# Next batch's rows normalised by ScalarE, result stores issued by ScalarE, and the work around them rearranged

## The chip, the cores and the metric

One core of a Trainium2 chip runs the whole program. The metric is device microseconds of one execution; the figure of a kernel is the median of several. The engines are TensorE (PE in the profile, PEld for its weight loads), VectorE (DVE), ScalarE (ACT), GpSimd (POOL) and SyncE (SP), which here only issues DMAs.

## The reference

Eight batches of 512 rows of 256 (`x`) attend to 1024 context rows each; then comes a feed-forward layer with routed experts. Cut to what matters:

```python
x = x + tanh(g_xattn) * xattn(layernorm(x), ctx)      # x 8x512x256, ctx 8x1024x256
x = x + tanh(g_ffn) * ffn(layernorm(x))
# xattn: lat, ctx = layer_norm(latents), layer_norm(context)
#   q = lat @ Wq; k, v = split(ctx @ Wkv); k = rope(k)        16 heads of 64
#   a = softmax(clip(q @ k.T / 8, -11, 11)); return (a @ v) @ Wo + bo
# ffn: scores = sigmoid(x @ router_w.T)                       64 experts in 8 groups
#   choose 4 groups, in them 8 experts per row; weights normed to sum 1, times 2.5
#   routed = sum over the chosen e of w_e * (relu(x @ up_w[e])**2 @ down_w[e])   256 -> 128 -> 256
#   shared = relu(x @ shared_up_w)**2 @ shared_down_w                            256 -> 512 -> 256
#   return routed + shared
```

## The kernel before

The program runs in four stages. Times are microseconds from the start of the span.

**Setup** (0 to 74) turns weights and the first batch's rows.

**Attention** (74 to 1905, function `attention`) goes over 8 batches `b`, in each over 8 pairs of heads `p`, in each over 8 steps `c`. In a step each engine's program runs its function `step`: TensorE multiplies `scores` (L903) for one tile of 128 context rows and both heads, and `ps_o` (L968, the product with `v`) for an earlier tile; ScalarE takes the exp into `e` (L1047); GpSimd clips `e` in place (L1139); VectorE sums `e` into `e_sum` (L1287), from which TensorE makes the denominators (L976). Beside this the next pair's keys are made: TensorE `ps_k` (L944), VectorE two products with cosines and sines, GpSimd their sum `k_c` (L1131, at c = 2 and 6), ScalarE the high part `k_t` (L1073), VectorE the rest of it (L1277). Batches 2 to 7 are one loop body, `Fori(2, B)`; batches 0 and 1 are written out.

Two more things are woven in. The next batch's rows (4 tiles of `x`, 8 of context) are layer-normalised in six groups of two tiles, one in each of the pairs 1 to 6: VectorE takes the moments at c = 0, GpSimd the inverse roots at c = 1 (`reciprocals`, L102), VectorE normalises at c = 6 (`Norms.normalise`, L90). And the batch before, whose attention is done, is routed: in `route`, VectorE adds the bias and takes statistics from (p, c) = (1,6) to (2,1), GpSimd takes inverse roots at (2,2), VectorE normalises two tiles of `rows_now` at (2,3) and two at (2,6) (`router.normalise`, L312), TensorE turns them over at (2,4) and (3,4) (`router.turn`, L320), ScalarE copies these at (2,5) and (3,5) (`router.copy`, L326), and logits, groups, ranks and gates follow to pair 7. The slots of its rows in the blocks of the experts are worked out by VectorE in the next batch's pair 0 (`finish_slots`). For the batch before that GpSimd scatters rows into DRAM (`scatter`, L1119), 32 indirect DMAs per batch of the loop at the steps that `places` lists, five in each of the pairs 1 to 6. ScalarE's keep of those rows (L561) is once per batch and marks its start.

**finish_routing** (1905 to 2051) routes the last batch and computes the shared expert for 8 groups of 512 rows. TensorE's order is: turn over group 0's rows, turn over the last batch's (L320), its logits (L340), then for each group four up products of two (L1426), the next group's turn and the down products (L1439).

**experts** (2051 to 2510) goes over 320 blocks of 128 rows. Blocks 0 to 63 are of expert i; those after take their expert from a table, and for these ScalarE copies its up weights (L1717). In TensorE's program a step i has the turn of block i (L1770, `ps_x`), the up products of block i−2 (L1739, `ps_hid`) and the down products of block i−4 (L1763, `ps_out`). ScalarE copies the turned rows (L1722) and half of the results (L1703, `keep`), VectorE takes relu (L1815) and square (L1819), the other results (L1795), and, for blocks under 84, parts of the gates (L1803 to L1808). SyncE issues, in this order for each i: x rows (L1661, two blocks, into a ring of 8), a chunk of four experts' down weights for i under 32 (L1681), and the store of four blocks' results (L1668), three fours behind:

```python
            for i in range(0, BLOCKS, XC):
                if i >= XR:
                    load(i)
...
                if i % YC == 0 and i >= 3 * YC:
                    store(i - 3 * YC)
```

From its block 112 on VectorE also adds one gathered result per block to the output (`combine`, L1788); GpSimd gathers them (L1844), 32 per batch, up to 8 ahead of the adding. The results' blocks end at 2451.7; 48 more are gathered and added behind.

## Time and profile before

| | |
|---|---|
| median of 3 runs | 2513.14 us (2508.35 to 2518.33) |
| profiled execution | 2512.1 us, its span 2510.3 us |
| TensorE busy | 2284.6 us (91%), mean granted clock 0.966 |
| VectorE | 2041.2 us (81%) |
| ScalarE | 1522.5 us (61%) |
| GpSimd | 1728.3 us (69%) |
| DMA | 306.26 MB, mean 122 GB/s |

The shares are means over stages with different limits, so they say only that TensorE is the engine with least to spare. What a stage waits for is read from its own stretch.

### The profile page before, as it was taken

To read this page: it belongs to the slowest core of one execution; us is meant where nothing else is said; L and a number is where in the kernel's file an instruction comes from. 1 tells how busy PE (TensorE), PEld (TensorE's weight loads), DVE (VectorE), ACT (ScalarE), POOL (GpSimd) and SP (SyncE) were. 2 spreads that over 40 slices of the span, in tenths; PEclk is the share of its full clock that TensorE was granted. 3 is DMA by queue.
4 is the path that set the end of the run, shared out by engine and by line. 5 is a ranking of instruction groups with operands and counts; after the bars stand their busy time and mean duration, and the time that the engine had idled before them with its cause. 6 is when DMAs were issued, how large, how long until landed. Compare 5 with 4: busy or idle time off the path is not lost. (4 is left out here: it accounts for less than half of the span.)

```text
span 2510.3 us, 40337 instructions
## 1 busy us (share of the span) xinstructions
PE 2284.6 (91%) x11366; PEld 1277.1 (51%) x11366; DVE 2041.2 (81%) x3571; ACT 1522.5 (61%) x2556; POOL 1728.3 (69%) x1515
## 2 busy tenths in 40 slices
PE   3999999999999999999999999999996989998990
PEld 2444445444444444454444444444544668987770
DVE  4778787988988898889889888988886759798884
ACT  4667666756666666667566756666662334766660
POOL 2777585588868876976788688868774600177776
PEclk9999999999999999999999999999997999999995
DMA  9533443111111112111112111111106438799994
GB/s 341 195 123 122 151 145 122 39 61 58 62 48 59 47 57 81 46 59 50 59 45 74 50 60 43 60 57 66 62 26 197 146 104 277 253 333 320 329 319 132
DMA packets 163582, 306.26 MB, mean 122 GB/s; under 512 B 19779, under 2 KB 99587, under 8 KB 160643
## 3 DMA queue, kind: packets, MB, share of 16 engines
q1 hardware_dynamic: 135234, 235.93, 27.5%
q0 software_dynamic: 24576, 67.14, 8.2%
q8 instruction: 105, 1.72, 0.3%
q14 instruction: 147, 1.20, 0.2%
q10 hardware_dynamic: 3520, 0.27, 0.1%
HBM read 173.51 MB, written 129.76 MB: 121 GB/s over the span
## 5 line engine op out<-in xcount | busy, mean ns | idle before, releaser
L1139 POOL TENSOR_SCALAR e<-e 128x1024 f32<-128x1024 f32 x512 | 706.9, 1381 | 320.7 <-ACT e L1047 267.5
L1047 ACT ACTIVATE e<-scores 128x1024 f32<-128x1024 f32 x512 | 524.7, 1025 | 424.3 <-PE scores L903 377.1
L1287 DVE TENSOR_TENSOR e_sum<-e_sum,e 128x1024 f32<-128x1024 f32 x384 | 589.7, 1536 | 100.7 <-POOL e L1139 100.4
L968 PE MATMUL ps_o<-e,v 128*64 128x512 f32 x2048 | 558.2, 624 | 7.8 <-POOL e L1139 7.7
L903 PE MATMUL scores<-q_t,k_t 64*128 64x512 f32 x3072 | 503.5, 433 | 15.1 <-DVE k_t L1277 11.8
L903 PEld LDWEIGHTS scores<-q_t,k_t 64*128 64x128 f32 x3072 | 253.4, 188 | 374.6 <-issue 282.7
L1844 POOL DMA_INDIRECT more<-results_in_blocks,index x256 | 246.0, 961 | 258.4 <-DMA results_in_blocks<-more 176.4
L1065 ACT ACTIVATE k_sw<-ps_k 32x512 f32<-32x512 f32 x512 | 301.3, 589 | 54.3 <-PE ps_k L944 49.2
L1119 POOL DMA_INDIRECT rows_in_blocks<-room,a_r_index_now x192 | 255.5, 1331 | 49.0 <-issue 49.0
L1131 POOL TENSOR_TENSOR k_c<-k_c,k_sw 128x512 f32<-128x512 f32 x128 | 192.6, 1505 | 46.7 <-DVE k_sw L1272 43.9
L944 PE MATMUL ps_k<-ctx_t,wqk 128*128 128x512 f32 x768 | 215.6, 417 | 0.9 <-DVE ctx_t L1163 0.3
L929 PE MATMUL ps_v<-wv,ctx_t 128*128 128x512 f32 x768 | 212.7, 412 | 2.4 <-ACT v L1058 2.4
L968 PEld LDWEIGHTS ps_o<-e,v 128*64 128x64 f32 x2048 | 102.1, 136 | 190.1 <-issue 156.3
L1763 PE MATMUL ps_out<-down_all,room 128*128 (+1 forms) x632 | 192.0, 386 | 0.7 <-DVE room L1819 0.3
L929 PEld LDWEIGHTS ps_v<-wv,ctx_t 128*128 128x128 f32 x768 | 135.0, 189 | 72.0 <-issue 45.5
L944 PEld LDWEIGHTS ps_k<-ctx_t,wqk 128*128 128x128 f32 x768 | 137.7, 193 | 65.8 <-issue 39.1
L1004 PE MATMUL ps_y<-wo,o_n 128*128 128x256 f32 x512 | 148.6, 414 | 13.2 <-DVE x L1210 9.6
L1739 PE MATMUL ps_hid<-x_nat,room 128*128 128x128 f32 x1024 | 157.3, 276 | 0.6 <-DVE room L1815 0.6
L1788 DVE SCALAR_TENSOR_TENSOR x<-more,gate,x 128x256 f32<-128x256 f32 x256 | 123.0, 480 | 42.5 <-DMA more<-results_in_blocks,index 41.5
L1722 ACT ACTIVATE x_nat<-ps_x 128x256 f32<-128x256 f32 x320 | 121.0, 379 | 59.4 <-PE ps_x L1770 56.0
L1277 DVE TENSOR_TENSOR k_t<-k_c,k_t 128x512 fp32r<-128x512 f32 x128 | 122.6, 958 | 41.2 <-ACT k_t L1073 41.0
L1004 PEld LDWEIGHTS ps_y<-wo,o_n 128*128 128x128 f32 x512 | 89.7, 195 | 130.4 <-issue 112.2
(288 smaller groups left out, 3510.5 us busy)
## 6 DMA issues: line engine op xcount, KB each, us to landing
rows_in_blocks<-room SPq DMA_DIRECT2D x16, 2560.0 KB, 10.5
x_nat<-rows_in_blocks SPq DMA_DIRECT2D x160, 256.0 KB, 5.3
results_in_blocks<-more SPq DMA_DIRECT2D x80, 512.0 KB
wqk<-wqk_pairs SPq DMA_DIRECT2D x65, 512.0 KB, 3.5
wv<-wv_quads SPq DMA_DIRECT2D x17, 1024.0 KB, 4.8
x_nat<-in_ctx SPq DMA_DIRECT2D x9, 1024.0 KB, 8.2
wo<-in_L_xattn_Wo SPq DMA_DIRECT2D x66, 128.0 KB, 3.4
down_all<-in_L_ffn_down_w SPq DMA_DIRECT2D x16, 512.0 KB, 7.7
```

The source lines that it names most:

```text
L903: mm = pe.matmul(scores[:, c % 2, hh * N:(hh + 1) * N], k_t[rows, att, kp, c * P:(c + 1) * P], q_t[rows, att, qp, :], start=(part == 0), s ...
L929: mm = pe.matmul(ps_v[:], ctx_t[:, a, cc, tile * P:(tile + 1) * P], wv[:, bb, cc], start=(k == 0), stop=(k == 5))
L944: mm = pe.matmul(ps_k[:], wqk[:, jj, bb, cc, 1], ctx_t[:, a, cc, half * N:(half + 1) * N], start=(k == 0), stop=(k == 5))
L968: mm = pe.matmul(ps_o[hh * DH:(hh + 1) * DH, :], v[:, tile, buf, hh * DH:(hh + 1) * DH], e[:, tile % 4, hh * N:(hh + 1) * N], start=(tile ...
L1004: mm = pe.matmul(ps_y[:, i, :], o_n[:, t * P:(t + 1) * P], wo[:, jj], start=True, stop=True)
L1047: act.activation(e[:, c % 4], scores[:, c % 2], ACT.Exp, scale=SCALE).then_inc(s_exp, 1)
L1065: st = act.activation(k_sw[to], ps_k[of], ACT.Copy)
L1119: pool.indirect_dma_start(xs_dram, bass.IndirectOffsetOnAxis(ap=router.index_now[:, t, k:k + 1], axis=0), router.rows[:, t], None).then_in ...
L1131: pool.tensor_tensor(k_c[:], k_c[:], k_sw[:], ALU.add).then_inc(s_turned, 1)
L1139: pool.tensor_scalar(e[:, c % 4], e[:, c % 4], EXP_HI, EXP_LO, ALU.min, ALU.max).then_inc(s_clip, 1)
L1287: dve.tensor_tensor(total, e[:, 0] if c == 2 else total, e[:, tile % 4], ALU.add).then_inc(s_sum, 1)
L1844: pool.indirect_dma_start(land[:, k], None, y_dram[0:blocks_of(b, k) * P, :], bass.IndirectOffsetOnAxis(ap=at, axis=0)).then_inc(y_in[k], 16)
```

## The change

1. The normalising of the next batch's rows leaves VectorE. GpSimd makes a bias, 0 − mean × rstd, with two more small operations per group; ScalarE applies scale and bias at c = 6 of pairs 1 to 6, ahead of its exp of that step's tile. Setup still uses VectorE.
2. The router's two turns stand at (3,3) and (3,4), their copies at (3,4) and (3,5); VectorE's first normalising moves from (2,3) to (2,4).
3. The scatter at (1,0) goes to (7,5), and GpSimd's wait for the slots moves from (1,0) to behind the clip of (1,1). The last part of the last-but-one batch's slots moves from step 7 to step 2 of the next pair.
4. `finish_routing` keeps its scratch in the memory of `down_all`, so the room of the first chunks can be filled early: 1 chunk when the rows are scattered, 3 after `last_kept`, 3 after the last turn; 9 are left to `experts`. TensorE does group 0's up products ahead of the router's turns and logits, ScalarE likewise.
5. In `experts` the stores of results are issued from ScalarE's program, two fours behind, and ScalarE takes relu for blocks 0 to 63, two blocks behind its copy.

The diff, cut to its core (each `...` leaves lines out; `rows_of(b, k)` gives the two tiles of group k as sources and places):

```diff
+    def normalise_on_act(self, act, sources, places, first, n_done):
+
+        pers = self.pers
+        act.wait_ge(self.rstd_done, n_done + 1)
+        for t, (src, dst) in enumerate(zip(sources, places)):
+            st = act.activation(dst, src, ACT.Identity, bias=pers.power[:, 3, first + t:first + t + 1],
+                                scale=pers.power[:, 2, first + t:first + t + 1])
+        st.then_inc(self.normed, 1)
...
             do(r, r, eps, ALU.add)
             do(r, r, minus_half, ALU.pow)
-            do(rr, r, rr, ALU.mult, True)
+            do(rr, r, rr, ALU.mult)
+        do(a, pers.moments[:, tiles, 0], rr, ALU.mult)
+        do(pers.power[:, 3, tiles], pers.zero[:].broadcast_to([P, n]), a, ALU.subtract, True)
...
@@ -977,16 +999,18 @@
                                        start=True, stop=True)
                     mm.then_inc(s_den, 1)
 
-                if routed(b) and c == 4 and p in (2, 3, 4, 6):
+                if routed(b) and ((p, c) == (3, 3) or c == 4 and p in (3, 4, 6)):
                     pe.wait_ge(s_rec, g + 1)
-                    if p in (2, 3):
-                        router.turn(pe, b - 1, p - 2, y_flat)
+                    if p == 3:
+                        if c == 4:
+                            pe.wait_ge(router.copied, (b - 1) * 2 + 1)
+                        router.turn(pe, b - 1, c - 3, y_flat)
                     elif p == 4:
                         router.logits(pe, b - 1, y_flat)
                     else:
                         router.rank(pe, b - 1, y_flat)
-                if routed(b) and c == 5 and p in (2, 3):
-                    pe.wait_ge(router.copied, (b - 1) * 2 + p - 1)
+                if routed(b) and c == 5 and p == 3:
+                    pe.wait_ge(router.copied, (b - 1) * 2 + 2)
                 if routed(b) and c == 5 and p == 4:
...
-                if routed(b) and c == 5 and p in (2, 3):
-                    router.copy(act, b - 1, p - 2, y_flat)
+                if routed(b) and p == 3 and c in (4, 5):
+                    router.copy(act, b - 1, c - 4, y_flat)
...
                     router.keep_moments(act, b - 1)
+                if project and c == 6 and 1 <= p <= ROW_GROUPS:
+                    norms.normalise_on_act(act, *rows_of(b, p - 1), b * ROW_GROUPS + p - 1)
...
-            places = [(p, c) for p in range(1, 7) for c in (0, 1, 4, 5, 7)] + [(7, 0), (7, 1)]
+            places = [(p, c) for p in range(1, 7) for c in (0, 1, 4, 5, 7)][1:] + [(7, 0), (7, 1), (7, 5)]
...
-                if (p, c) == (1, 0) and not isinstance(b, int):
-                    pool.wait_ge(router.slotted, b - 1)
-                    pool.wait_ge(router.rows_kept, b - 1)
...
                 if p is not None and not isinstance(b, int) and (p, c) in places:
+                    if (p, c) == places[0]:
+                        pool.wait_ge(router.slotted, b - 1)
+                        pool.wait_ge(router.rows_kept, b - 1)
+                        pool.sem_inc(s_seen, 1)
                     scatter(b, places.index((p, c)))
...
+                if 1 <= p <= ROW_GROUPS and c == 0:
+                    rows, places, first = rows_of(b, p - 1)
+                    if p == 3:
                         dve.wait_ge(x_loaded, (b + 1) * 16)
-                    if c == 0:
-                        norms.moments_of(dve, rows, first, b * ROW_GROUPS + k)
-                    else:
-                        norms.normalise(dve, rows, places, first, b * ROW_GROUPS + k)
+                    norms.moments_of(dve, rows, first, b * ROW_GROUPS + p - 1)
...
-                if (p, c) == (2, 3):
+                if (p, c) == (2, 4):
                     router.normalise(dve, 0)
...
-                if attend and not project and c in FINISH:
+                if attend and not project and c in FINISH[:-1]:
                     finish_slots(B - 2, FINISH.index(c))
+                if not attend and not project and c == 2:
+                    finish_slots(B - 2, len(FINISH) - 1)
...
+        x_last = sb([P, GT, D])
+        assert taken_up == ROWS_END * CHUNK * D
+        router.scratch(lambda name, shape, dt=F32: sb(shape, dt), None, x_last)
+        assert taken_up <= ROUTING_END * CHUNK * D
+        taken_up = ROUTING_END * CHUNK * D
+        x_nat = sb([P, RING * GT, D]).rearrange("p (r t) n -> p r t n", t=GT)
+        assert taken_up == RING_END * CHUNK * D
+        x_f = sb([P, 2, C2, TG])
+        router.x_f = x_f[:, 1]
...
+        def load_down(sp, chunks):
+            for k in chunks:
+                sp.dma_start(down[:, k * CHUNK:(k + 1) * CHUNK],
+                             ins["down_w"][k * CHUNK:(k + 1) * CHUNK].rearrange("e p n -> p e n")).then_inc(kept.down_loaded[k], 16)
...
-            sp.dma_start(router.rows, ins["down_w"][0:CHUNK].rearrange("e p n -> p e n")).then_inc(kept.first_loaded, 16)
+            load_down(sp, range(0, ROWS_END))
+            sp.wait_ge(last_kept, 1)
+            load_down(sp, range(ROWS_END, ROUTING_END))
             for i in range(0, XR, XC):
                 sp.dma_start(pers.x_nat[:, i:i + XC], four_blocks(xs_dram, i)[:, i % YC:i % YC + XC]).then_inc(kept.x_loaded[i // XC], 16)
             sp.wait_ge(table_in, 16)
+            sp.wait_ge(x_turned, N_G * C2)
+            load_down(sp, range(ROUTING_END, RING_END))
...
             turn(0)
+            ups(0)
             router.turn(pe, last, 0, ps_r[:])
             router.turn(pe, last, 1, ps_l[:])
             router.logits(pe, last, ps_r[:])
-            for g in range(N_G):
-                if g == 1:
-                    router.rank(pe, last, ps_l[:])
-                shared(g)
+            downs(0)
+            router.rank(pe, last, ps_l[:])
+            for g in range(1, N_G):
+                ups(g)
+                downs(g)
...
-            router.copy(act, last, 0, ps_r[:])
-            router.copy(act, last, 1, ps_l[:])
-            router.tanh(act, last, ps_r[:])
             for g in range(N_G):
                 shared(g)
+                if g == 0:
+                    router.copy(act, last, 0, ps_r[:])
+                    router.copy(act, last, 1, ps_l[:])
+                    router.tanh(act, last, ps_r[:])
...
-                e = i // XC * CHUNK
+                e = (i // XC + RING_END) * CHUNK
...
-                if i % YC == 0 and i >= 3 * YC:
-                    store(i - 3 * YC)
...
-            for i in range(BLOCKS - 3 * YC, BLOCKS, YC):
-                store(i)
...
+            def store(i):
+                for parity in range(2):
+                    act.wait_ge(s_y[parity], (i + YC) // 2)
+                act.dma_start(four_blocks(y_dram, i),
+                              y[:, i % YR:i % YR + YC]).then_inc(y_stored[i % YR // YC], 16)
+
             for i in range(BLOCKS):
+                if i % YC == 0 and i >= 2 * YC:
+                    store(i - 2 * YC)
...
+                j = i - 2
+                if 0 <= j < E_R:
+                    act.wait_ge(s_up, j + 1)
+                    if j >= 2:
+                        act.wait_ge(s_g, j - 1)
+                    act.activation(act_r[:, j % 2], ps_h[:, j % 2, 0:P], ACT.Relu).then_inc(s_relu, 1)
             keep(BLOCKS - 4)
+            store(BLOCKS - 2 * YC)
             keep(BLOCKS - 2)
+            store(BLOCKS - YC)
...
-                dve.wait_ge(s_up, i + 1)
-                dve.tensor_scalar(act_r[:, i % 2], ps_h[:, i % 2, 0:P], 0.0, None, ALU.max).then_inc(s_relu, 1)
+                if i >= E_R:
+                    dve.wait_ge(s_up, i + 1)
+                    dve.wait_ge(s_g, i - 1)
+                    dve.tensor_scalar(act_r[:, i % 2], ps_h[:, i % 2, 0:P], 0.0, None, ALU.max).then_inc(s_relu, 1)
```

What the change moves on three engines. First TensorE in the loop's body, pair 2, steps 3 to 5, before (`ident` is the identity by which rows are turned over, `e` the exps, `wo` the output weights):

```order
L944 MATMUL ps_k<-ctx_t,wqk 128x512 x6
L968 MATMUL ps_o<-e,v 64x512 x2
L317 ISA
L320 MATMUL ps_y<-ident,rows_now 128x128 x4
L894 REGISTER_ALU
L903 MATMUL scores<-q_t,k_t 128x512 x6
L968 MATMUL ps_o<-e,v 64x512 x2
L997 REGISTER_ALU
L1004 MATMUL ps_y<-wo,o_n 128x256 x2
```

The same place in the changed kernel (its lines are some 22 higher), without the turn:

```order
L961 REGISTER_ALU
L966 MATMUL ps_k<-ctx_t,wqk 128x512 x6
L990 MATMUL ps_o<-e,v 64x512 x2
L916 REGISTER_ALU
L925 MATMUL scores<-q_t,k_t 128x512 x6
L990 MATMUL ps_o<-e,v 64x512 x2
L1021 REGISTER_ALU
L1028 MATMUL ps_y<-wo,o_n 128x256 x2
```

and its pair 3, steps 3 and 4, which now has both:

```order
L925 MATMUL scores<-q_t,k_t 128x512 x6
L990 MATMUL ps_o<-e,v 64x512 x2
L329 ISA
L332 MATMUL ps_y<-ident,rows_now 128x128 x4
L916 REGISTER_ALU
L925 MATMUL scores<-q_t,k_t 128x512 x6
L961 REGISTER_ALU
L966 MATMUL ps_k<-ctx_t,wqk 128x512 x6
L990 MATMUL ps_o<-e,v 64x512 x2
L329 REGISTER_ALU
L332 MATMUL ps_y<-ident,rows_now 128x128 x4
L916 REGISTER_ALU
```

So the four turned tiles stand behind each other in pair 3, with a step's scores and products between, and nothing of them in pair 2.

Second, GpSimd in pair 2, step 1, the powers for a group of `x` rows, in the changed kernel (`power` is the strip in which the inverse roots are made; lines L112 are L102 before):

```order
L112 TENSOR_TENSOR power<-power,minus_half 128x2
L115 REGISTER_ALU
L112 TENSOR_TENSOR power<-power 128x2
L115 REGISTER_ALU
L112 TENSOR_TENSOR power<-moments,power 128x2
L115 REGISTER_ALU
L112 TENSOR_TENSOR power<-zero_d,power 128x2
L1152 ISA
L1153 TENSOR_TENSOR k_c<-k_c,k_sw 128x512
L1159 REGISTER_ALU
L1161 TENSOR_SCALAR e<-e 128x1024
```

Before, the rows are the same without those with `moments,power` and `zero_d,power`. The sum `k_c` and the clip of `e` stand behind them.

Third, the experts. ScalarE's program for blocks under 64, before (L1703 copies a result, L1722 turned rows):

```order
L1703 ACTIVATE more<-ps_out 128x256
L1722 ACTIVATE x_nat<-ps_x 128x256 x2
L1703 ACTIVATE more<-ps_out 128x256
L1722 ACTIVATE x_nat<-ps_x 128x256 x2
L1703 ACTIVATE more<-ps_out 128x256
L1722 ACTIVATE x_nat<-ps_x 128x256 x2
```

and after (L1743 copies a result, L1770 turned rows, L1776 is relu, L1748 issues the store):

```order
L1743 ACTIVATE more<-ps_out 128x256
L1770 ACTIVATE x_nat<-ps_x 128x256
L1776 ACTIVATE room<-ps_hid 128x128
L1748 DMA results_in_blocks<-more 128x1024
L1770 ACTIVATE x_nat<-ps_x 128x256
L1776 ACTIVATE room<-ps_hid 128x128
L1743 ACTIVATE more<-ps_out 128x256
L1770 ACTIVATE x_nat<-ps_x 128x256
L1776 ACTIVATE room<-ps_hid 128x128
L1770 ACTIVATE x_nat<-ps_x 128x256
L1776 ACTIVATE room<-ps_hid 128x128
```

SyncE's queue at the same blocks, before:

```order
L1681 DMA down_all<-in_L_ffn_down_w 128x4x256
L1668 DMA results_in_blocks<-more 128x1024
L1661 DMA x_nat<-rows_in_blocks 128x512
L1681 DMA down_all<-in_L_ffn_down_w 128x4x256
L1661 DMA x_nat<-rows_in_blocks 128x512
L1681 DMA down_all<-in_L_ffn_down_w 128x4x256
L1668 DMA results_in_blocks<-more 128x1024
L1661 DMA x_nat<-rows_in_blocks 128x512
```

SyncE keeps the x rows and the down chunks, and a store no longer stands between them.

## Rows read from the trace of the kernel before

**Rows 1.** Busy times by stage, with TensorE's granted clock; first row names the columns.

```profile
core 0: us, PE busy (x) PEld busy (x) DVE busy (x) ACT busy (x) POOL busy (x), PEclk, DMA share, GB/s
74.00:1905.00 1831.00, 1752.13 (x8198) 844.89 (x8194) 1555.87 (x2164) 1192.13 (x1670) 1394.11 (x1146) 0.98 0.21 71
1905.00:2051.00 146.00, 130.84 (x489) 88.52 (x488) 95.63 (x223) 51.16 (x87) 67.75 (x71) 0.92 0.45 146
2051.00:2133.40 82.40, 73.64 (x497) 64.08 (x498) 70.22 (x200) 32.86 (x95) 0.00 (x0) 0.96 0.85 288
...
2191.00:2451.70 260.70, 238.74 (x1650) 205.59 (x1648) 226.79 (x727) 168.62 (x513) 198.16 (x206) 0.99 0.95 321
```

**Rows 2.** ScalarE's L561: durations min/median/max in ns, first and last start.

```profile
L561 ACT ACTIVATE room<-rows_now x7: 1047/1053/1055, 480.5 to 1866.4; 128x1024 f32<-128x1024 f32 x7
```

**Rows 3.** Head pairs 2 and 3 of one batch, columns as in rows 1.

```profile
1003.40:1033.70 30.30, 26.14 (x118) 11.60 (x116) 25.05 (x39) 16.60 (x24) 26.59 (x26) 0.89 0.13 46
1033.70:1058.60 24.90, 23.71 (x118) 10.52 (x116) 22.11 (x26) 17.64 (x27) 22.89 (x19) 1.00 0.17 58
```

**Rows 4.** Timeline of TensorE: start, us, ..., [idle before <-what ended it].

```profile
326.46 1.09 PE L320 MATMUL ps_y<-ident,rows_now 128*128 128x128 f32 x4 [3.40 <-DVE rows_now L312]
...
1017.58 1.11 PE L320 MATMUL ps_y<-ident,rows_now 128*128 128x128 f32 x4 [3.12 <-DVE rows_now L312]
...
1058.59 1.08 PE L976 MATMUL ps_y<-e_sum,ones_dh 128*64 128x512 f32 x4 [1.19 <-DVE e_sum L1287]
```

**Rows 5.** Timeline of GpSimd in pair 2.

```profile
1009.21 0.19 POOL L102 TENSOR_TENSOR power<-power,eps 128x2 f32<-128x2 f32 x1
...
1010.91 1.28 POOL L1131 TENSOR_TENSOR k_c<-k_c,k_sw 128x512 f32<-128x512 f32 x1
...
1016.34 2.68 POOL L1139 TENSOR_SCALAR e<-e 128x1024 f32<-128x1024 f32 x2
```

**Rows 6.** Timeline of all engines around a key's making in pair 3.

```profile
1050.82 2.44 DVE L90 TENSOR_SCALAR x_nat<-x_nat,moments,power 128x256 f32<-128x256 f32 x2
...
1051.81 1.29 POOL L1131 TENSOR_TENSOR k_c<-k_c,k_sw 128x512 f32<-128x512 f32 x1
...
1053.13 0.63 ACT L1073 ACTIVATE k_t<-k_c 128x512 fp32r<-128x512 f32 x1 [2.04 <-POOL k_c L1131]
...
1053.80 0.97 DVE L1277 TENSOR_TENSOR k_t<-k_c,k_t 128x512 fp32r<-128x512 f32 x1 [0.54 <-ACT k_t L1073]
```

**Rows 7.** L90 in one batch: busy us, mean ns, idle before.

```profile
L90 DVE TENSOR_SCALAR x_nat<-x_nat,moments,power 128x256 f32<-128x256 f32 x8 | 7.2, 937 | 0.0
```

**Rows 8.** Timeline of TensorE, end of attention and start of finish_routing.

```profile
1894.42 1.98 PE L976 MATMUL ps_y<-e_sum,ones_dh 128*64 128x512 f32 x4 [3.30 <-DVE e_sum L1287]
...
1915.91 1.12 PE L320 MATMUL ps_r<-ident,x_last 128*128 128x128 f32 x4 [3.53 <-DVE x_last L312]
...
1922.03 9.70 PE L1426 MATMUL ps_h<-x_f,sup 128*128 128x512 f32 x16
```

**Rows 9.** Timeline of TensorE: turns of the blocks 8, 64 and 112.

```profile
2062.13 0.69 PE L1770 MATMUL ps_x<-ident,x_nat 128*128 128x128 f32 x2 [4.04 <-DMA x_nat<-rows_in_blocks]
...
2133.39 0.38 PE L1770 MATMUL ps_x<-ident,x_nat 128*128 128x128 f32 x2
...
2186.15 0.38 PE L1770 MATMUL ps_x<-ident,x_nat 128*128 128x128 f32 x2
```

**Rows 10.** Timeline in blocks under 64: VectorE's relu, ScalarE's copy.

```profile
2076.57 0.28 DVE L1815 TENSOR_SCALAR room<-ps_hid 128x128 f32<-128x128 f32 x1
...
2102.42 0.38 ACT L1722 ACTIVATE x_nat<-ps_x 128x256 f32<-128x256 f32 x1 [0.66 <-PE ps_x L1770]
```

**Rows 11.** What TensorE's turns of blocks waited for: us, times.

```profile
  DMA x_nat<-rows_in_blocks: 69.2, 67
```

**Rows 12.** Timeline of GpSimd: first gather from block 112 on, and last.

```profile
2191.05 0.94 POOL L1844 DMA_INDIRECT more<-results_in_blocks,index  x1 [7.64 <-DVE x L1788]
...
2503.74 0.94 POOL L1844 DMA_INDIRECT more<-results_in_blocks,index  x1 [0.30 <-issue]
```

More of the change, by code:

```diff
@@ L113, in reciprocals @@
         do(a, var, eps, ALU.add)
-        do(rr, a, minus_half, ALU.pow, not latent)
+        do(rr, a, minus_half, ALU.pow)
         if latent:
@@ L736, in attention @@
         rows_now = sb("rows_now", [P, GT, D])
-        router.scratch(nc, ctx, "a_", affine[:], rows_now[:])
+        router.small(sb)
+        router.scratch(sb, affine[:], rows_now[:])
         minus_gate = sb("minus_gate", [P, 1])
@@ L1606, in _, with experts @@
             shared(7)
-def experts(nc, pers, ins, out, kept, router, up, xs_dram, y_dram):
+def experts(nc, pers, ins, out, kept, router, up, down, xs_dram, y_dram):
     with ExitStack() as ctx:
@@ L1632, in experts @@
         ps_y = ctx.enter_context(nc.psum_tensor("ps_out", [P, 4, N], F32))
-        down_loaded = [sem(f"down_loaded_{k}") for k in range(E_R // CHUNK)]
+        down_loaded = kept.down_loaded
         x_loaded = kept.x_loaded
@@ L1663, in load @@
                              ).then_inc(x_loaded[i % XR // XC], 16)
-            def store(i):
-                for parity in range(2):
-                    sp.wait_ge(s_y[parity], (i + YC) // 2)
-                sp.dma_start(four_blocks(y_dram, i),
-                             y[:, i % YR:i % YR + YC]).then_inc(y_stored[i % YR // YC], 16)
             def finish(b):
@@ L1877, in program @@
         up = ctx.enter_context(nc.sbuf_tensor("up_all", [P, E_R, D], F32))
-        finish_routing(nc, pers, ins, kept, router, up, xs_dram, table_dram, slots_dram, gates_dram)
-        experts(nc, pers, ins, out, kept, router, up, xs_dram, y_dram)
+        down = ctx.enter_context(nc.sbuf_tensor("down_all", [P, E_R, D], F32))
+        finish_routing(nc, pers, ins, kept, router, up, down, xs_dram, table_dram, slots_dram, gates_dram)
+        experts(nc, pers, ins, out, kept, router, up, down, xs_dram, y_dram)
 def kernel(**inputs):
```

100 lines of the change are left out of this document (51 added, 49 removed).

## The prediction

> **What bounds the kernel now.** I read the busy times by stage first [rows 1]. In attention TensorE is busy 1752.13 of 1831.00 us, in the last batch's routing 130.84 of 146.00. These two stages go by TensorE, and only its waits, or a lower granted clock, can give anything back. In the first 82.4 us of the experts TensorE (73.64) and VectorE (70.22) stand close together. From 2191 us VectorE (226.79 of 260.70) and GpSimd (198.16, with the gaps between its gathers not counted) rival TensorE.
>
> Then I read where attention's batches start [rows 2]: from 480.5 to 1866.4 us in six equal steps of 231.0 us, so one batch stands for all. In it TensorE waits mainly in head pairs 2 and 3 [rows 3]: 30.30 us with 26.14 busy at a clock of 0.89 of the full one, then 24.90 us with 23.71 busy. The waits have names [rows 4]: 3.12 us for `rows_now`, the router's normalised rows, and 1.19 for `e_sum`. GpSimd is busy 26.59 of 30.30 us and 22.89 of 24.90 there, in 26 and 19 instructions with a gap of some 0.1 to 0.3 us behind each. So in pair 2 it is as full as it can be.
>
> For the experts I read when TensorE starts blocks 8, 64 and 112 [rows 9], and the gathers at both ends [rows 12].
>
> **The change part by part.** The sum is made against the profiled execution, 2512.1 us (span 2510.3), which is 1.0 below the median 2513.14.
>
> (a) Batches 2 to 7. VectorE loses 12 normalisations per batch: 7.2 us in the eight of context rows [rows 7] and at most as much each in the four others. ScalarE takes them, 12 instructions that no trace here shows; its pass over 128x512 lasts 0.63 us [rows 6], VectorE's over 128x256 0.94, so 0.35 to 0.95 us each, 4 to 11 us per batch. ScalarE is busy 16.60 and 17.64 us in these pairs [rows 3], which hides them if they don't stand in front of a late exp. GpSimd gains two operations on 128x2 in each of six groups, 0.19 us each [rows 5] and with a gap of at most (30.30 − 26.59)/26 = 0.14 us [rows 3], so 0.4 to 0.7 us per pair. The router's first turn leaves (2,4), where TensorE waited 3.12 us for it.
>
> I cost the turn's wait at nothing gained. Removing it doesn't give TensorE its next `ps_o` matmuls: these need the clipped `e`, and GpSimd starts the pair of clips at 1016.34 and ends it 2.68 us later [rows 5], the first of them about when the rows came (1017.58). GpSimd is held by its own list, the norm powers, `k_c`, the router's powers and the scatters, not by TensorE. I also cost VectorE's relief at nothing in pairs 2 and 3. Around 1051 us `k_t` goes from GpSimd's `k_c` (ends 1053.10) to ScalarE (1053.76) to VectorE (1054.77) [rows 6]: VectorE waited for both. What is late next is `e`, and behind it `e_sum`, for which TensorE waits again. So what is left is GpSimd's extra work: +0.5 in pair 2, +0.5 in pair 3, a little in the other pairs, less some 0.4 of slack. The second turn and the first now both stand in pair 3, but that moves TensorE's work and adds none. I take +1 us per batch, six times: **+6**. Bounds per batch: all of 3.12 and 1.19 back and some 2 us of lower clock and 1 us of smaller waits with them, −7.3; or GpSimd's additions in full plus a late exp behind a ScalarE normalisation (0.95), +2.5.
>
> The Trainium skill speaks against a flat reading here. Its page "SBUF — State Buffer", section "Who interferes with whom", says that VectorE and GpSimd share a port pair as an exclusive lock, taken by a VectorE operation in a two-port mode, such as a tensor_scalar, or by one with two SBUF inputs against a GpSimd one that reads. By it each L90 that goes would free GpSimd. The trace gives little for it: `k_c` beside a running L90 took 1.29 us [rows 6], and an earlier one without it 1.28 [rows 5].
>
> (b) Batch 1 has the turn but no scatters on GpSimd. Its wait is 3.40 us [rows 4], and GpSimd's list is shorter, so the wait mostly goes: **−3** (0 to −5, with the clock).
>
> (c) The tail of attention: the last part of the slots leaves VectorE's way ahead of an `e_sum` for which TensorE waits 3.30 us [rows 8]. Half of it: **−1.7** (0 to −3.3).
>
> (d) The last batch's routing. TensorE waits 3.53 us for `x_last` and a few tenths more ahead of the logits; then the 16 up matmuls of group 0 run 9.70 us [rows 8]. With these put into the gap, up to 4.2 us go, less about 1.5 for `x_f`, which ScalarE still copies, and with TensorE cold as before: **−2.7** (0 to −7, if those matmuls also run faster).
>
> (e) Experts, blocks 0 to 63. Blocks 8 to 63 take 2133.39 − 2062.13 = 71.3 us, 1.27 each. Blocks 64 to 111 take 52.8 us, 1.10 each [rows 9]. VectorE's relu lasts 0.28 us and starts the next operation 0.32 later [rows 10]. Without it VectorE's cycle is 1.27 − 0.32 = 0.95, and TensorE's 1.10 would show: at most (1.27 − 1.10) × 56 = 9.7. ScalarE's cycle becomes a copy of 0.38 [rows 10], half a second one (0.19), a relu of 0.28 to 0.38 and the store's issue and wait: 0.85 to 0.95 without gaps, perhaps 1.15 with them, which would leave 6.9. Of the wait of 4.04 us for x rows ahead of block 8 I give nothing back: four down chunks still stand in front of these rows on SyncE's queue. Three more down chunks stand ahead of the first x rows, in a stage whose DMA share is 0.45 [rows 1]; I cost them at nothing, and if the x rows land late for it, by up to the same 4.04 us again. I take **−6** (−3 to −9.7).
>
> (f) From block 112. The gathers start at 2191.05, the last of these at 2503.74 [rows 12], 247 steps of 0.95 + 0.30 = 1.25 us are 309.0 of the 312.7 between: 3.6 us of waits in all. TensorE's 69.2 us of waits for x rows [rows 11] lie beside this chain. The stores' new issuer can end those waits and gain nothing: **−0.6** (0 to −3.6). Behind a store on ScalarE's program stand its copies and the weight copies; the store needs VectorE's share of block i−5 at ScalarE's block i, due about a block earlier, so I cost its wait at nothing; if that cover is gone, ScalarE's copies come late and all of TensorE with them.
>
> The Trainium skill's page "DMA: Bandwidth & Descriptors", section "Issuing engines are not separate DMA queues", says that DMAs from several engines run on the same 16 DMA engines and that spreading them saves only the issuing time. The DMA share is already 0.95 in that stretch [rows 1]; the same bytes move after.
>
> Sum: 6 − 3 − 1.7 − 2.7 − 6 − 0.6 = −8.0, so 2512.1 − 8.0 = 2504.1.
>
> **The rivals.** Forecast: attention flat or a little slower, the rest −8 to −14, giving 2496 to 2512: chance 0.42.
>
> Rival 1: the turn's wait really goes. With scores issued 3 us earlier, exp and clips follow earlier, TensorE keeps its clock, and GpSimd catches up in the scatters' gaps. Between −2.5 and −6 per batch, times six, −15 to −36, with the rest −14: 2463 to 2490, most likely near 2480. For it: the clock of 0.89 in pair 2 against 1.00 in pair 3 [rows 3]. Against it: GpSimd's 26.59 busy plus gaps. Chance 0.28.
> By the Trainium skill's rule on the lock VectorE's lighter load would push the same way.
>
> Rival 2: the gains of routing and experts are taken back at the next wait (the first gather, x rows landing behind the earlier down chunks), or attention costs +2 to +2.5 per batch: 2512 to 2523. Chance 0.18.
>
> Rival 3, slower: ScalarE becomes the bound of the experts. It needs a cycle per block above GpSimd's 1.25 us, that is over 5.0 us per four blocks with the store's wait in it; from there each further 0.1 us per block costs 0.1 × 208 = 21 us over blocks 112 to 319, less the 8.0 of the sum. 0.12 us over the limit already gives 2504 + 25 = 2529. For it: ScalarE is busy 168.62 of 260.70 us [rows 1], 0.81 per block, before the store. Against it: 0.44 us per block is left. Range 2526 to 2560. Chance 0.12.
>
> **How the numbers follow.** A measurement here tells about 0.5% from no change: under 2500.6 is faster, over 2525.7 slower. Faster: all of rival 1 (0.28) and a third of the forecast (0.14), 0.42. Slower: 0.12. Same: 0.46. The forecast's own range is 2496 to 2512. For 8 in 10 it goes down to 2476, which leaves out a quarter of rival 1, and up to 2522, which leaves out rival 3 and little of rival 2.
>
> **What would show it.** Right: the batches' steps are 231 to 233 us; TensorE has no wait for `rows_now` in pair 2 but waits of the same size for `e` or `e_sum`; GpSimd's busy time in pair 2 is 27; block 64 starts some 65 us after block 8; the gathers run at 1.25 us from the first to the last. Wrong: a step of 226 to 229 us with pair 2's clock near 1.00 (rival 1), or waits of ScalarE for `more` or of TensorE for its copies in blocks 112 to 319 (rival 3).

## The result and the profile after

The changed kernel takes 2527.95 us (median of 4, 2526.92 to 2528.95) against 2511.93 us in the same comparison; the ratio is 1.0064, 95% interval 1.0051 to 1.0077. That is 16 us slower, where 2504 was forecast and 2476 to 2522 given as the range. It lies outside that range, inside the 2526 to 2560 of rival 3, and just over the 0.5% that I had called slower; to each of these two I gave 0.12.

The stages of the changed kernel's profiled execution (span 2525.8 us), in the columns of [rows 1]; its times lie later, so the stretches are cut at its own marks below:

```profile
74.00:1905.00 1831.00, 1745.64 (x8191) 838.46 (x8190) 1485.17 (x2054) 1236.18 (x1767) 1401.96 (x1240) 0.99 0.21 71
1905.00:2051.00 146.00, 128.04 (x476) 84.42 (x477) 98.30 (x235) 51.26 (x88) 69.40 (x73) 0.93 0.51 169
```

VectorE is 71 us less busy in attention than in [rows 1], and no time came of it. The batches, by ScalarE's keep (answers to [rows 2]):

```profile
L573 ACT ACTIVATE room<-rows_now x7: 1048/1051/1057, 481.4 to 1877.1; 128x1024 f32<-128x1024 f32 x7
```

The last keep is 10.7 us later than before, the first 0.9, so the six batches between them lost 9.8. The steps are not equal, as the prediction read them from the first and the last start: before they are 232.8, 232.1, 232.0, 232.1, 231.9 and, for the batch that prepares no next one, 225.1; after, 233.5, 234.8, 233.2, 234.6, 233.1 and 226.5. Then TensorE's turns of blocks 8, 64 and 112 (answers to [rows 9]), and GpSimd's first gather from there and its last (to [rows 12]):

```profile
2067.18 0.69 PE L1822 MATMUL ps_x<-ident,x_nat 128*128 128x128 f32 x2 [3.64 <-DMA x_nat<-rows_in_blocks]
2136.75 0.38 PE L1822 MATMUL ps_x<-ident,x_nat 128*128 128x128 f32 x2
2194.54 0.38 PE L1822 MATMUL ps_x<-ident,x_nat 128*128 128x128 f32 x2
```

```profile
2199.24 0.94 POOL L1898 DMA_INDIRECT more<-results_in_blocks,index  x1 [9.04 <-DVE x L1840]
...
2519.20 0.95 POOL L1898 DMA_INDIRECT more<-results_in_blocks,index  x1 [0.30 <-issue]
```

| stretch | before | after | difference |
|---|---|---|---|
| to the loop's first keep | 480.5 | 481.4 | +0.9 |
| six batches | 1385.9 | 1395.7 | +9.8 |
| last keep to TensorE's first turn of the last routing (1910.41, 1917.82) | 44.0 | 40.7 | −3.3 |
| to block 8 | 151.7 | 149.4 | −2.3 |
| block 8 to block 64 | 71.3 | 69.6 | −1.7 |
| block 64 to block 112 | 52.8 | 57.8 | +5.0 |
| block 112 to the last gather | 317.6 | 324.7 | +7.1 |

So the six batches lost 10, and the experts from block 8 on, where I had −6.6, lost 10 as well. Each stretch is read from one execution. The traces with the attention of before, or with only a scatter moved (before, runs 2, 11 and 6 below), have 1385.9 to 1390.3 us for the six batches, and those with the changed one (the changed kernel, runs 1, 3 and 12) 1394.8 to 1396.6, so the 10 is clear of that spread.

**Attention.** Pairs 2 and 3 of the batch of [rows 3], and TensorE's waits there (to [rows 4]):

```profile
1008.20:1038.60 30.40, 23.37 (x112) 10.09 (x108) 23.99 (x32) 18.18 (x26) 26.73 (x28) 1.00 0.14 48
1038.60:1064.00 25.40, 24.38 (x120) 11.01 (x120) 19.77 (x24) 18.05 (x28) 23.30 (x21) 1.00 0.16 52
```

```profile
1018.94 1.08 PE L990 MATMUL ps_o<-e,v 128*64 128x512 f32 x4 [1.85 <-POOL e L1161]
...
1038.60 1.08 PE L998 MATMUL ps_y<-e_sum,ones_dh 128*64 128x512 f32 x4 [1.91 <-DVE e_sum L1303]
```

The 3.12 us for the rows are gone, the clock in the pair is full, and the pair is as long as before: TensorE waits for the clipped `e` and for its sum. In every other batch pair 3 takes 26.0 us. Busy time counts longer at a lower clock, so its 25.94 are the same work as the 24.38 above:

```profile
803.50:829.50 26.00, 25.94 (x120) 11.69 (x120) 20.41 (x24) 17.43 (x27) 23.32 (x21) 0.93 0.14 46
```

The prediction looked at pairs 2 and 3 alone. In the kernel before pair 7 holds more waiting than pair 3, most of it for the key's last part:

```profile
1145.40:1176.70 31.30, 27.77 (x136) 13.88 (x138) 27.49 (x34) 23.11 (x34) 19.66 (x15) 0.95 0.09 28
```

```profile
1169.46 1.62 PE L903 MATMUL scores<-q_t,k_t 64*128 64x512 f32 x6 [2.92 <-DVE k_t L1277]
```

From one denominator of pair 1 to the next, the batches 2 to 6 take 233.2, 235.1, 232.8, 235.1 and 232.8 us after the change, and 231.9 to 232.4 before. The three short ones lost 0.8 or 0.9 each: 0.5 in pair 3, 0.3 in pair 6, 0.1 in pair 2. The two long ones lost 2.2 more, at lower clocks: 0.6 in pair 3 and 1.6 in pair 7 (32.9 or 33.0 us at 0.90, where the others have 31.1 to 31.6 at 0.95).

**Experts.** ScalarE's timeline at one store, in blocks 64 to 111 (ACTq is its own DMA queue's issue):

```profile
2160.16 0.41 ACT L1765 ACTIVATE room<-up_all 128x256 f32 x1
2160.47 0.38 ACT L1770 ACTIVATE x_nat<-ps_x 128x256 f32<-128x256 f32 x1
2161.59 0.33 ACTq L1748 DMA_DIRECT2D results_in_blocks<-more  x1
2162.47 0.42 ACT L1765 ACTIVATE room<-up_all 128x256 f32 x1 [1.62 <-PE ps_hid L1795]
2162.79 0.36 ACT L1770 ACTIVATE x_nat<-ps_x 128x256 f32<-128x256 f32 x1
```

and VectorE and TensorE beside it:

```profile
2160.35 0.60 PE L1815 MATMUL ps_out<-down_all,room 128*128 x2
...
2161.08 0.42 DVE L1847 COPY more<-ps_out 128x256 f32<-128x256 f32 x1
...
2163.30 0.41 PE L1822 MATMUL ps_x<-ident,x_nat 128*128 128x128 f32 x2 [0.15 <-ACT x_nat L1770]
```

The reader sees ScalarE stop at 2160.85. The store waits until VectorE has written the fourth result (2161.50), is issued at 2161.59, and the next weights' copy starts 0.88 us later. Of the 1.62 us that ScalarE stands idle 0.74 are the wait and 0.88 the issue with the table word's load behind it. The program's order says why the wait is there at every store from block 64 on: ScalarE comes to the store of block i straight from its copy of the turned rows of block i−1, and the down products of block i−5, whose result the store needs, are TensorE's last work of that same step i−1. They end at 2160.95, after ScalarE has stopped, and VectorE's copy of them comes behind. The row names `ps_hid` as releaser, but that product was long done: a wait that the view put down to the wrong one, found by the rows of the other engines. TensorE then waits for ScalarE's copies, a thing that [rows 11] and the page of before have only as exceptions. From block 64 on:

```profile
its engine sat idle before it (us, times) until:
  issue: 55.4, 65
  ACT x_nat L1770: 31.0, 63
```

The `issue` row is the weight load of the same turns, which stands idle together with them, so the two aren't to be added. The waits for x rows that [rows 11] counted are gone from here (in the same view of the kernel before, from 2141 to 2464 us, they are 53.1 us in 59 places), as the prediction said they might be, and ScalarE's stand in their place.

### The profile page after: what moved, and what is told of

It is laid out like the page before. It is cut to its first block and busy times, and to the rows that moved or that the text cites. A ratio compares the mean times of both kernels' runs of the same rounds, so it can differ in the third digit from the quotient of the medians.

```text
span 2525.8 us, 40882 instructions
## 1 busy us (share of the span) xinstructions
PE 2280.5 (90%) x11366; PEld 1263.4 (50%) x11366; DVE 1960.6 (78%) x3411; ACT 1564.0 (62%) x2716; POOL 1741.5 (69%) x1616
## 5 line engine op out<-in xcount | busy, mean ns | idle before, releaser
L1161 POOL TENSOR_SCALAR e<-e 128x1024 f32<-128x1024 f32 x512 | 690.8, 1349 | 319.7 <-ACT e L1071 291.2
L990 PE MATMUL ps_o<-e,v 128*64 128x512 f32 x2048 | 555.3, 621 | 31.3 <-POOL e L1161 31.3
L1144 POOL DMA_INDIRECT rows_in_blocks<-room,r_index_now x192 | 256.7, 1337 | 50.7 <-issue 47.4
L1153 POOL TENSOR_TENSOR k_c<-k_c,k_sw 128x512 f32<-128x512 f32 x128 | 182.2, 1423 | 41.3 <-DVE k_sw L1288 38.3
L1293 DVE TENSOR_TENSOR k_t<-k_c,k_t 128x512 fp32r<-128x512 f32 x128 | 128.0, 1000 | 101.8 <-ACT k_t L1097 101.8
L1765 ACT ACTIVATE room<-up_all 128x256 f32 x256 | 106.7, 417 | 126.1 <-PE ps_hid L1795 112.6
L1822 PE MATMUL ps_x<-ident,x_nat 128*128 128x128 f32 x640 | 124.8, 277 | 41.1 <-ACT x_nat L1770 36.1
```

The source lines that it names most:

```text
L990: mm = pe.matmul(ps_o[hh * DH:(hh + 1) * DH, :], v[:, tile, buf, hh * DH:(hh + 1) * DH], e[:, tile % 4, hh * N:(hh + 1) * N], start=(tile ...
L1144: pool.indirect_dma_start(xs_dram, bass.IndirectOffsetOnAxis(ap=router.index_now[:, t, k:k + 1], axis=0), router.rows[:, t], None).then_in ...
L1161: pool.tensor_scalar(e[:, c % 4], e[:, c % 4], EXP_HI, EXP_LO, ALU.min, ALU.max).then_inc(s_clip, 1)
```

## The experiments

All were timed in five rounds against the kernel before (2511.6 to 2513.6 us in the three comparisons).

**1. stores_back_on_sync.** The changed kernel with

```diff
-                if i % YC == 0 and i >= 2 * YC:      # ScalarE's program
-                    store(i - 2 * YC)
+                if i % YC == 0 and i >= 3 * YC:      # SyncE's, between the x rows
+                    store(i - 3 * YC)
```

> The changed kernel with the stores of results issued by SyncE again, three fours behind, at the old place between x rows. Theory A (ScalarE's program stands at each store until VectorE's share of the four results is written, then issues it and loads the table word, and its copies come late for TensorE): blocks 64 to 111 go from 57.8 us back to about 52.8, and from block 112 to the last gather from 324.7 to about 317.6, so 12 us less in all, about 2516 us. Rival B (the stretch is due to what DMA moves earlier, the down chunks, or to the waits added to VectorE's relu): these two stretches stay at 57.8 and 324.7, and the time at 2528.

Measured 2511.23 us, ratio to before 0.9996 (0.9987 to 1.0005), 16.7 less than the changed kernel. Block 64 to 112 takes 52.9 us, 112 to the last gather 318.0, and blocks 8 to 63 take 64.0 in place of 69.6, which I had not expected: the store had been eating most of relu's gain too. The stretch from block 64 in this kernel, with TensorE busy throughout, and in the changed one:

```profile
2133.70:2186.50 52.80, 52.80 (x385) 47.86 (x384) 35.40 (x118) 39.79 (x124) 7.63 (x8) 1.00 0.77 253
```

```profile
2136.80:2194.50 57.70, 55.20 (x385) 47.02 (x384) 35.16 (x118) 37.05 (x122) 7.74 (x8) 1.00 0.72 237
```

Rival B falls. The edit changes two things together, the issuer and the distance (three fours behind in place of two); no run has ScalarE's store at another distance.

**2. only_stores_on_act.** The same edit the other way round, alone in the kernel before.

> The kernel before with nothing changed but the issuer of the stores, ScalarE's program, two fours behind. Theory A: blocks 64 to 111 take 57.8 us in place of 52.8, block 112 to the last gather 324.7 in place of 317.6; about 2524 us, 12 above before. Rival B: no change, 2512.

Measured 2523.33, ratio 1.0041 (1.0028 to 1.0055). Block 64 to 112: 57.2 us; to the last gather 323.3. The store alone costs some 11 us in the kernel before, none of it in blocks 8 to 63 (70.4 us after 71.3), where ScalarE has no relu here.

**3. store_behind_weights_copy.** The changed kernel with the store moved down within the step, behind ScalarE's result copy, the table word and the weights' copy:

```diff
                                    ).then_inc(s_now, 1)
+                if i % YC == 0 and i >= 2 * YC:
+                    store(i - 2 * YC)
                 act.wait_ge(s_turn, i + 1)
```

> The changed kernel with ScalarE's store moved down within the same step, behind its result copy, the table word and the weights' copy, and ahead of the copy of the turned rows. Theory A: the wait for VectorE then lies behind 0.4 to 1.0 us of ScalarE's own work and most of the 1.6 us of standing still per four blocks goes; blocks 64 to 111 take 53 to 54.5 us and the whole 8 to 12 us less than the changed kernel, 2516 to 2520. If what costs is the issue of the DMA on ScalarE's program itself (0.33 us and what follows it), and not the wait, the place matters little: 2525 to 2528.

Measured 2515.53, ratio 1.0008 (0.9997 to 1.0019), 12.4 less than the changed kernel. Blocks 64 to 111 take 53.1 us. ScalarE's timeline there:

```profile
2151.63 0.42 ACT L1763 ACTIVATE room<-up_all 128x256 f32 x1
...
2152.49 0.33 ACTq L1748 DMA_DIRECT2D results_in_blocks<-more  x1
...
2152.92 0.38 ACT L1770 ACTIVATE x_nat<-ps_x 128x256 f32<-128x256 f32 x1 [0.87 <-PE ps_hid L1795]
```

It stands 0.87 us in place of 1.62, with the weights' copy and the table word already done, and TensorE goes on without a wait. Over all blocks behind its waits for ScalarE's copies come to 8.6 us, in the changed kernel to 31.0. So from block 64 on the issue on ScalarE's program is bearable, and its place is what costs. In blocks 8 to 63, where no weights are copied and the store stays right ahead of the turned rows' copy, nothing is gained: 69.6 us.

**4. normalise_on_vector_again.** The changed kernel with part 1 undone.

> The changed kernel with part 1 undone: VectorE normalises the next batch's rows at step 6, and GpSimd makes no bias (12 small operations less per batch). Theory C (in attention GpSimd's added operations are what costs): a batch of the loop goes from 232.8 or 235.0 us down to about 232, some 9 us less in all, about 2519. Rival D (ScalarE's normalisations ahead of the exp cost it): the same sum, but then the wait moves from the exps in pairs 3 and 6. Rival E (the moved turn costs it): batches stay at 232.8 and 235.0 and the time at 2528.

Measured 2522.75, ratio 1.0038 (1.0025 to 1.0052), 5.2 less than the changed kernel. The batches stay at 233 to 235 us (233.2, 234.8, 233.1, 234.7, 232.9 from one denominator of pair 1 to the next, against 233.2, 235.1, 232.8, 235.1, 232.8), except pair 6, 26.1 us in place of 26.4, and pair 3, which now takes 25.9 or 26.0 at a clock of 0.93 or 0.94 in every batch. Theory C falls here, and E is favoured. Of the 4.1 us by which its profiled execution is shorter 3.0 lie in the experts, which this kernel does not change, so they tell nothing.

**5. only_turn_moved.** The kernel before with part 2 alone (`(p, c) == (3, 3)` in place of (2,4), and what goes with it).

> The kernel before with part 2 alone: the router's first turn at (3,3), its copies at (3,4) and (3,5), VectorE's first normalising at (2,4). If the turn is what lengthens attention (theory T), batches go from 232.0 to about 233.1, mainly by the pair with the first gap (24.9 to 26.0 us), and the time to about 2518. If GpSimd alone sets pair 2 and nothing else suffers (my forecast's reading), batches stay at 232.0 and the time at 2512. If the wait for the rows really were worth its size, 229 and 2495.

Measured 2520.69, ratio 1.003 (1.0014 to 1.0046), batches of 233.1 to 234.5 in place of 232.0. TensorE's waits in its pair 2, and the windows of its pair 3:

```profile
1019.24 1.90 PE L968 MATMUL ps_o<-e,v 128*64 128x512 f32 x4 [2.08 <-POOL e L1141]
1035.48 1.08 PE L976 MATMUL ps_y<-e_sum,ones_dh 128*64 128x512 f32 x4 [2.21 <-DVE e_sum L1289]
```

```profile
1035.50:1061.40 25.90, 25.82 (x120) 11.96 (x120) 21.86 (x26) 16.55 (x25) 22.54 (x19) 0.93 0.13 44
```

Pair 2 stays at 30.3: what stood as 3.12 us at the turn stands at `e` and at the pair's end. Pair 3 takes 25.8 to 27.3 us in five of six batches, with a clock of 0.88 to 0.94, where [rows 3] have 24.9 at 1.00. In the sixth its clock is full:

```profile
801.80:826.70 24.90, 24.34 (x118) 10.96 (x118) 22.04 (x26) 16.86 (x26) 22.96 (x19) 1.00 0.16 53
```

So the four turns more, 0.6 us of work, fit into the time that TensorE had waited there, and the 1 us that the pair grows elsewhere goes with the lower clock behind the later wait. That one batch still takes 233.7 us, since its pair 7 has 33.0 at 0.90.

**6. only_scatter_moved.** The kernel before with `places` and the wait of part 3.

> The kernel before with the first half of part 3 alone: no scatter at (1,0), one at (7,5), and GpSimd's wait for the slots behind the clip of (1,1). Theory S: a scatter of 1 to 1.9 us ahead of the key's sum of (7,6) delays the key in the pair where TensorE already waits for it, so pair 7 goes from 31.3 to 33 us in some batches, batches from 232.0 to 232.8 to 233.6 and the time up by 5 to 10 us. Rival: GpSimd is idle a third of pair 7, so nothing changes, 2512.

Measured 2512.59, ratio 1.0 (0.9989 to 1.0011). The rival holds. Single batches of its trace do show pair 7 at 32.9 or 32.5 us, others 31.2. So does the changed kernel; pair 7 of two of its batches:

```profile
1151.10:1182.30 31.20, 27.87 (x136) 13.87 (x138) 27.86 (x34) 22.82 (x34) 20.63 (x16) 0.95 0.09 32
1384.50:1417.30 32.80, 28.92 (x134) 14.30 (x136) 27.87 (x34) 23.19 (x34) 19.93 (x16) 0.90 0.11 35
```

TensorE waits 3.3 us in one and 3.9 in the other (the stretch less its busy time), which is a third of the 1.6 between them; the rest is busy time, 27.87 against 28.92, at a clock of 0.95 and 0.90. What I had put down to the scatter is mostly a lower granted clock around a wait of the same kind. It needs no change of attention either: run 2, whose attention is that of before, has two batches with pair 7 at 32.5 us and 0.90; there pair 2 is shorter by nearly as much (29.4 or 29.5 us at 0.94).

**7 and 8. sync_stores_old_turn, sync_stores_old_turn_and_scatter.** The changed kernel with stores on SyncE and the turn back at (2,4); in the second the scatter and its wait go back too.

> The changed kernel with the stores issued by SyncE and the turn back at (2,4). Theory T: against stores_back_on_sync (2511) it gains what the turn costs, about 1 us per batch, so 2505; if the scatter at (7,5) is what costs, 2511.

> The changed kernel with the stores issued by SyncE, the turn back at (2,4), and the scatter and GpSimd's wait back at (1,0). Everything in attention but the normalising and the tail is then as before: batches near 232 us in all, with the tail's 3, the 2 of the last routing and the 7 of blocks 8 to 63 kept, about 2498 to 2502. If ScalarE's normalising costs by itself, batches stay above 232.5 and the time above 2504.

Measured 2523.61, ratio 1.0044 (1.003 to 1.0058), and 2522.28, ratio 1.004 (1.0027 to 1.0054). Both were missed by some 20 us: the batches rise to 235.5 us. With the turn at its old place part 1 costs 3.5 us per batch; with the turn moved it costs next to nothing (run 4). The parts don't add up, and theory E of run 4, that the moved turn is what costs, holds for the kernel before (run 5) and not for the changed one.

**9. only_bias_made.** The kernel before, in which GpSimd makes the bias and nobody reads it:

```diff
+        do(a, pers.moments[:, tiles, 0], rr, ALU.mult)
+        do(pers.power[:, 3, tiles], pers.zero[:].broadcast_to([P, n]), a, ALU.subtract, True)
```

> The kernel before, in which GpSimd also makes the bias (12 more operations on 128x2 per batch) that nobody reads; VectorE still normalises. Theory G (GpSimd's added operations delay the clips in pairs 2 and 3): pair 2 goes from 30.3 to 31.1 us, pair 3 from 24.9 to about 26, the batch from 232.0 to about 234.5, the time to about 2527. If ScalarE's normalising is what delays (theory N), nothing: 232.0 and 2512.

With them come two more waits of GpSimd for its own results, as it has between the others. Measured 2531.53, ratio 1.0075 (1.0061 to 1.0089), 20 us for 12 operations of 0.19 us per batch; batches of 234.9 to 235.5. Theory G holds. Its pair 2 on TensorE and on GpSimd:

```profile
1023.00 1.08 PE L972 MATMUL ps_o<-e,v 128*64 128x512 f32 x4 [1.88 <-POOL e L1143]
1027.20 1.11 PE L323 MATMUL ps_y<-ident,rows_now 128*128 128x128 f32 x4 [3.12 <-DVE rows_now L315]
```

```profile
1015.95 1.71 POOL L103 TENSOR_TENSOR power<-power,minus_half 128x2 f32<-128x2 f32 x1
...
1020.13 0.20 POOL L103 TENSOR_TENSOR power<-moments,power 128x2 f32<-128x2 f32 x1
1020.40 0.20 POOL L103 TENSOR_TENSOR power<-zero_d,power 128x2 f32<-128x2 f32 x1
```

The two take 0.27 us each from start to start, and the powers ahead of them another 0.2 more than before (one `pow` takes 1.71 us where it took 0.72, another 0.69 where it took 1.21; what stretches them no run shows). So the clip behind them starts 9.7 us into the pair in place of 8.9, TensorE's wait for it is 0.9 longer than before's (0.94), and the wait for the rows stays whole behind it, since they too come from GpSimd. The pairs: 31.4 in place of 30.3, 25.3 in place of 24.9, 26.6 in place of 26.1, and 32.7 in place of 31.3 in pair 7, where GpSimd makes no bias at all:

```profile
1156.30:1189.00 32.70, 29.07 (x136) 14.30 (x138) 28.00 (x35) 23.23 (x33) 19.61 (x15) 0.90 0.10 31
```

TensorE waits 3.6 us there, in the kernel before 3.5 (31.30 less 27.77); the clock is 0.90 there and was 0.95. So the clock makes the difference, now in every batch of the loop that has a next one. Batch 0, which routes nothing and has the full clock, takes 217.7 us after 216.7: that 1.0 is what the operations cost without the clock and the router.

**10. only_normalise_on_scalar.** Part 1 whole, in the kernel before.

> The kernel before with part 1 whole: GpSimd's bias and ScalarE's normalising ahead of the exp of step 6. From sync_stores_old_turn_and_scatter (235.5 us per batch): 235.5, some 3.5 per batch and 20 in all more than before, 2532. Theory G says that nearly all of this is already in only_bias_made; theory N that it appears only here.

Measured 2533.43, ratio 1.0088 (1.0072 to 1.0103), batches of 235.6. In sum VectorE's relief of some 9 us per batch and ScalarE's 12 normalisations of 0.59 us come to nothing beyond the bias. The sum hides a shift: pair 3 takes 26.4 us here and 25.3 in run 9, pair 7 31.5 to 32.4 here and 32.5 to 32.8 there. As both engines change together, a gain of the one can stand against a cost of the other.

**11. best_of_both.** The changed kernel with stores on SyncE and parts 1, 2 and the first half of 3 undone.

> The changed kernel with stores on SyncE and with parts 1, 2 and the first half of 3 undone, so attention as before but for the tail. It keeps the tail (3.4 us), the last routing (2) and blocks 8 to 63 (7): 2512 less 12, about 2500, batches at 232.0.

Measured 2502.68 us (2498.97 to 2504.54), ratio 0.9961 (0.9948 to 0.9975): 9 us faster than the kernel before and 25 faster than the changed one. Its batches are back at 232.0 to 232.3, one at 233.9 (pair 7 at 33.1 us and 0.90); blocks 8 to 63 take 64.1 us. It differs from run 8 by part 1 alone, and that is worth some 20 us.

**12. sync_stores_relu_on_vector.** Run 1's kernel with relu on VectorE for all blocks.

> The changed kernel with stores on SyncE and relu on VectorE for all blocks. If relu on ScalarE is what shortens blocks 8 to 63 (64.0 us in stores_back_on_sync against 71.3 before), they take 71 again and the time is 7 more, 2518; if the down chunks loaded early do it, they stay at 64 and the time at 2511.

Measured 2518.46, ratio 1.0026 (1.0017 to 1.0036), 7.2 more than run 1. Blocks 8 to 63 take 70.2 us. It is relu, and in these blocks the early down chunks give at most the 1.1 us that are left to 71.3. Ahead of them this kernel's TensorE waits 2.32 us for the x rows of block 8, run 1's 3.68 and before's 4.04; no run has the early chunks alone.

## Why the prediction was wrong

The step that failed most is in (f): "the store needs VectorE's share of block i−5 at ScalarE's block i, due about a block earlier, so I cost its wait at nothing". "About a block earlier" is what was wrong: in TensorE's order the down products of block i−5 close the step in which ScalarE comes to the store. VectorE's copy ends 0.65 us after that, every four blocks, and 0.88 us of issue and table load follow. Undoing it gave 16.7 us. Of the 23.4 us between the forecast and the profiled execution (2527.49 − 2504.1), 12.7 lie in the stretches from block 64 on, for which −0.6 stood, 4.3 in blocks 8 to 63, 3.8 in the six batches and 3.9 before them, less 1.2 between attention and block 8. I had the mechanism as rival 3 and sized it wrongly: its point of decision, 5.0 us per four blocks, was taken from ScalarE's mean load and from GpSimd's 1.25 us. What counts is not the mean but how late the turned rows' copy is, and in blocks 64 to 111 the rate to keep was TensorE's 1.10. There each store costs 0.42 us ((57.8 − 52.8)/12); in the steady part, block 128 to 288, 208.7 us against 202.9 of run 1, it costs 0.15. That is less than my 25 us and more than nothing. That the time fell into rival 3's range is in part luck: its limit of 5.0 us per four blocks was not what was passed, and attention added its share.

(e) The mechanism was right and the term near: relu on ScalarE gives 70.2 − 64.0 = 6.2 us with the stores elsewhere (run 12 against run 1), forecast 6. In the change it showed only 1.7, because the same ScalarE also had the store. I had put both into one cycle of "perhaps 1.15" per block and then counted the gain once and the store nowhere.

(a) The forecast said +6 for six batches; they came to +9.8. Three of the batches 2 to 6 lost the 0.8 or 0.9 us that were forecast as 1, though in pairs 3 and 6 and not in pair 2; the two others lost 3.0 each, and what they have more stands at lower clocks, most of it in pair 7, which the prediction left out. The reading that held: removing the turn's wait gives nothing, since TensorE then waits for `e` and `e_sum`; pair 2 stayed at 30.4 and rival 1 is refuted by steps of 233 to 235 us, though the clock rose in pair 2 to 1.00 as that rival wanted. The sentence "that moves TensorE's work and adds none" left out the clock: the turn alone cost 1.4 us per batch (run 5), nearly all of it at clocks below 1.00 in pairs 3 and 7, while the work itself fitted into pair 3's waits. And two operations that I had at 0.5 us per pair cost 3.4 us per batch in the kernel before (run 9): 1.1 in pair 2, 0.4 in pair 3, 0.5 in pair 6 and 1.4 in pair 7, where none of them stands and the clock is lower. In batch 0 the changed kernel loses 1.3 us (218.0 after 216.7), which is part 1 without any routing; the prediction had no term for batch 0. In the loop of the changed kernel, with the turn moved, the two operations cost nearly nothing (run 4). Why just this pair of edits cancels, I only read from the waits (the clip is late in both, but the rows' wait no longer adds to it); no run shows it apart, and so this cause stays open.

(b) −3 was forecast, and batch 1, from its pair 2 to the next batch's, took 225.6 us after 226.3. The wait moved here as it did in the loop: in pair 2 TensorE waits 0.94 and 2.60 us for `e`, in place of 0.42 for `e` and 3.40 for the rows.

(c) The tail gave 3.3 us where −1.7 stood. The wait for `e_sum` gave the half that was forecast (1.79 us after 3.30), and the wait for `x` ahead of it shrank as well (1.60 us after 3.66). (d) The last routing, from its first turn to the first block (1917.82 to 2056.65 after, 1910.41 to 2051.19 before), gave 2.0 where −2.7 stood. The parts of this stage and of the tail were not run apart.

By the rule of the shared port pair that the prediction took from the Trainium skill's page "SBUF — State Buffer", section "Who interferes with whom", each L90 that goes would free GpSimd. With those of attention gone GpSimd's 512 clips take 691.5 us (run 10) after 695.1 (run 9), and the batches are no shorter. The trace of before shows the two in each other's way, but in most of these meetings it is VectorE that takes longer: an L90 with neither a clip nor `k_c` beside it took 0.40 us, others up to 2.12, while the clips that began 1 to 20 ns behind such an L90 took their usual 1.04 and the `k_c` beside the longest 1.27 to 1.29. Four of the five clips that began 70 to 101 ns behind an L90 took 1.21 to 1.23 and left it at 0.41.

```profile
L90 DVE TENSOR_SCALAR x_nat<-x_nat,moments,power x72: 398/448/2119, 31.0 to 1835.9; 128x256 f32<-128x256 f32 x72
```

What the page "DMA: Bandwidth & Descriptors" of the Trainium skill says of issuing engines fits these runs: in blocks 64 to 111 the DMA engines moved 253 GB/s with the stores on SyncE (run 1) and 237 with them on ScalarE. It says that spreading saves issuing time; here the issue on ScalarE cost time.

## What to carry to other kernels

A DMA store in a compute engine's program brings its wait with it: read where the last of its producers ends against the time at which that engine arrives, at each store and not on average, and put the store behind whatever others need first. A wait that is taken away from one place can stand again at the next, and the granted clock around it can change: compare busy times only at equal clocks, and look at every batch, not at one. And small operations ahead of what TensorE waits for can cost more than their length, so test such edits alone and in pairs: here two edits that cost 1.4 and 3.4 us per batch cost 1.6 together, and the best version drops both.

## What the runs showed of the hardware

A ScalarE activation with scale and bias over 128x256 took 0.59 us in each of its 96 places (0.587 to 0.598, run 10). VectorE's tensor_scalar over the same took 0.40 us undisturbed and up to 2.12 beside GpSimd's scatters, clips and `k_c`, 0.94 in the mean of [rows 7]. From the issue of a DMA on ScalarE's program to the next activation it took 0.43 us (run 3), and 0.88 with a table word's load between.

Waits of TensorE of the same size and at the same place went with different clocks: with waits of 3.5 and 3.6 us pair 7 took 31.3 us at a mean granted clock of 0.95 in the kernel before and 32.7 at 0.90 in run 9, which is 1.4 us more. Pair 3 of the changed kernel took 25.4 at 1.00 or 26.0 at 0.93, alternating from batch to batch, behind a pair 2 of 30.4 us in both. Within one kernel, whose batches run the same code, this varies.
